# Weights turned in one pass, products of constants in TensorE's early waits, layer-norm pieces in other periods

## What is computed

```python
def _layernorm(x, axis=-1, eps=1e-05):
    m = jnp.mean(x, axis=axis, keepdims=True)
    v = jnp.var(x, axis=axis, keepdims=True)
    return (x - m) / jnp.sqrt(v + eps)
...
    Q = jnp.einsum('bnd,hdk->bhnk', x, proj_q)
    K = jnp.einsum('bmd,dk->bmk', x, proj_k)
    V = jnp.einsum('bmd,dv->bmv', x, proj_v)
    logits = jnp.einsum('bhnk,bmk->bhnm', Q, K)
    weights = jax.nn.softmax(logits, axis=-1)
    O = jnp.einsum('bhnm,bmv->bhnv', weights, V)
    Y = jnp.einsum('bhnv,hdv->bnd', O, proj_o)
...
    mid = jnp.einsum('amh,ehn->aemn', x, w1)
    out = jnp.einsum('aemn,enh->amh', mid, w2)
...
    xn = _layernorm(x, axis=-1)
    x = x + attention(xn) + ffn(xn)
```

## Time and profile before

| | us |
|---|---|
| median of 3 runs | 1669.87 |
| lowest, highest | 1668.98, 1670.22 |
| time of the profiled execution | 1669.67 |
| its span in the trace | 1667.9 |
| TensorE busy | 1634.7 |
| GpSimd busy | 1379.9 |
| ScalarE busy | 1304.2 |
| VectorE busy | 1239.3 |

### The profile page before, as it was taken

How to read it: one execution, slowest core, us unless ns; L and a number is a source line. 1 busy time by engine, 2 the same in 40 slices (tenths; PEclk the granted TensorE clock), 3 DMA queues, 4 the chain that set the end, 5 groups by cost and what they waited for, 6 DMA issues and landing times.

```text
span 1667.9 us, 46510 instructions
## 1 busy us (share of the span) xinstructions
PE 1634.7 (98%) x18820; PEld 1214.1 (73%) x18820; DVE 1239.3 (74%) x2655; ACT 1304.2 (78%) x1350; POOL 1379.9 (83%) x1008
## 2 busy tenths in 40 slices
PE   7999999999999999999999999999999999999998
PEld 6777777777777777777777777777777777777775
DVE  5777777777777777777777777777777777777775
ACT  4777877787787788778778777877878787787785
POOL 2788888888888888888888888888888888878876
PEclk9999999999999999999999999999999999999999
DMA  8000000000000000000000000000000000000000
GB/s 230 2 2 2 1 2 14 2 2 2 2 15 2 2 2 3 13 2 2 2 8 8 2 2 1 8 8 2 2 2 8 8 2 2 2 14 2 2 1 14
DMA packets 16769, 16.73 MB, mean 10 GB/s; under 512 B 432, under 2 KB 12976, under 8 KB 16560
## 3 DMA queue, kind: packets, MB, share of 16 engines
q1 hardware_dynamic: 15520, 13.24, 2.7%
q10 hardware_dynamic: 1040, 0.52, 0.1%
HBM read 9.57 MB, written 4.19 MB: 8 GB/s over the span
## 4 chain that ended last, share of the span: by engine, by line
POOL 56%; issue 24%; PE 18%; ACT 1%; DVE 0%; POOLq 0%; DMA 0%; SPq 0%; DVEq 0%; ACTq 0%
POOL pr_lo L306 40%; POOL xacc L318 9%; POOL xn L300 3%; PE s_ps L548 2%; PE s_ps L550 2%; PE s_ps L535 2%; PE t_ps L586 2%; PE t_ps L589 2%; PE t_ps L588 2%; POOL rstd L345 2%; POOL xacc L324 1%; POOL xn_lo L290 1%; PE s_ps L432 1%; PE s_ps L434 1%; PE s_ps L433 1%
## 5 line engine op out<-in xcount | busy, mean ns | idle before, releaser
L306 POOL TENSOR_TENSOR pr_lo<-pr,pr_hi 128x1024 f16<-128x1024 f32 x511 | 1086.4, 2134 | 264.3 <-ACT pr_hi L396 264.3
L389 ACT ACTIVATE pr<-s_ps,boost,scale 128x1024 f32<-128x1024 f32 x512 | 616.8, 1205 | 211.1 <-PE s_ps L550 210.3
L778 DVE TENSOR_REDUCE key_max<-s_ps 128x128 f16<-128x1024 f32 x512 | 624.0, 1219 | 0.0
L396 ACT ACTIVATE pr_hi<-pr 128x1024 f16<-128x1024 f32 x512 | 525.4, 1051 | 8.1
L548 PE MATMUL s_ps<-g_lo,xT 128*128 128x128 f16 x4096 | 512.4, 219 | 1.1 <-DVE g_lo L791 1.1
L550 PE MATMUL s_ps<-g_hi,xT 128*128 128x128 f16 x4096 | 512.3, 219 | 0.0
L548 PEld LDWEIGHTS s_ps<-g_lo,xT 128*128 128x128 f16 x4096 | 400.7, 98 | 31.6 <-DVE g_lo L791 1.6
L550 PEld LDWEIGHTS s_ps<-g_hi,xT 128*128 128x128 f16 x4096 | 400.8, 98 | 29.7
L586 PE MATMUL t_ps<-pr_hi,xn_hi 128*128 128x512 f16 x1024 | 388.7, 380 | 16.3 <-POOL pr_lo L306 14.4
L588 PE MATMUL t_ps<-pr_lo,xn_hi 128*128 128x512 f16 x1024 | 388.1, 379 | 0.0
L589 PE MATMUL t_ps<-pr_hi,xn_lo 128*128 128x512 f16 x1024 | 388.1, 379 | 0.0
(11 more groups left out here) (123 smaller groups left out, 1602.7 us busy)
## 6 DMA issues: line engine op xcount, KB each, us to landing
out_dram<-xacc SPq DMA_DIRECT2D x16, 256.0 KB, 2.3
w_sb<-in_L_ffn_w_dram SPq DMA_DIRECT2D x1, 2048.0 KB, 10.2
pr<-in_L_attn_proj_q_dram ACTq DMA_DIRECT2D x1, 512.0 KB, 4.7
xacc<-in_L_attn_x_dram SPq DMA_DIRECT2D x2, 256.0 KB, 5.1
pr<-in_L_attn_proj_o_dram SPq DMA_DIRECT2D x1, 512.0 KB, 6.5
xacc<-in_L_attn_x_dram SPq DMA_DIRECT2D x1, 384.0 KB, 11.0
xacc<-in_L_attn_x_dram SPq DMA_DIRECT2D x1, 128.0 KB, 6.3
wkv<-in_L_attn_proj_k_dram SPq DMA_DIRECT2D x1, 64.0 KB, 2.9
```

Of the source, the lines that this page charges most:

```text
L306: pool.tensor_tensor(pr_lo[:, u % RING, :], pr32[:, u % PR, :], pr_hi[:, u % RING, :], ALU.subtract)\
L389: act.activation(pr32[:, u % PR, :], both_banks(u), ACT.Exp, bias=boost[:, 0:1], scale=scale[:, 0:1])\
L396: act.activation(pr_hi[:, u % RING, :], pr32[:, u % PR, :], ACT.Copy).then_inc(p_hi_ready, 1)
L778: dve.tensor_reduce(key_max[:, u % 2, :], both_banks(u).rearrange("p (t q) -> p q t", q=P), AX_X, ALU.max).then_inc(keys_max, 1)
```

## The change

1. Turns: wq, wo and w1 are turned by `pe.transpose` with ident, which is one instruction in place of two. Since this no longer centres, wq is centred by VectorE (a copy of the first column, then a subtraction that also empties the bank), and F is centred once by a product in period 7. w1 is turned in periods 0 to 3 into one bank, emptied by ScalarE and VectorE in turn; all of F is folded in periods 4 and 5.
2. `keep_going`: 24 products of constants (6, 5, 8 and 5), 512 columns each, at four places of TensorE's queue ahead of the loop. Nothing reads their result.
3. Start-up order: a_hi is made for head 0 alone first; C is folded in two halves around the first scores; the emptying of wq's turn, the low part of the first tiles and others go to other engines or places; the first projection comes ahead of the second turn of x.
4. Layer norm of coming tiles: rstd in period 8p+8, normalise in 8p+9, xn_hi on ScalarE in 8p+10, xn_lo in 8p+11. Statistics have two slots. VectorE's pieces stay in their periods.

The core of the diff:

```diff
+        def ln_slot(tile):
+
+            return AHEAD + tile % 2
...
+            first_rstd(0)
+            first_rstd(1)
+            xn_low(0, 0, HT)
             xn_low(HT, HT, HT)
+            first_rstd(2)
...
-                if n % 8 == 2 and (tile := ln_tile(n // 8)) is not None:
-                    pool.wait_ge(ln_var, tile - AHEAD + len(FIRST_TILES) + 1)
-                    pool.tensor_tensor(rstd[:, AHEAD:AHEAD + 1], var_eps[:, AHEAD:AHEAD + 1],
-                                       minus_half[:, 0:1], ALU.pow).then_inc(ln_rstd, 1)
-                if n % 8 == 3 and (tile := ln_tile(n // 8)) is not None:
-                    normalise_next(tile)
-                if n % 8 == 7 and (tile := ln_tile(n // 8)) is not None:
-                    xn_low(tile, 0, 1)
+
+                if (tile := ln_tile(n // 8 - 1)) is not None:
+                    if n % 8 == 0:
+                        slot = ln_slot(tile)
+                        pool.wait_ge(ln_var, tile - AHEAD + len(FIRST_TILES) + 1)
+                        pool.tensor_tensor(rstd[:, slot:slot + 1], var_eps[:, slot:slot + 1], minus_half[:, 0:1], ALU.pow)\
+                            .then_inc(ln_rstd, 1)
+                    if n % 8 == 1:
+                        normalise_next(tile)
+                    if n % 8 == 3:
+                        xn_low(tile, 0, 1)
...
-                if n % 8 == 6 and (tile := ln_tile(n // 8)) is not None:
+                if n % 8 == 2 and (tile := ln_tile(n // 8 - 1)) is not None:
                     split_high(tile, 0, 1)
...
+            def keep_going(count):
+
+                for n in range(count):
+                    pe.matmul(sum_bank(0).rearrange("p (n c) -> p n c", c=P), ident16[:, :],
+                              ident16[:, :].unsqueeze(1).to_broadcast([P, 4, P]), start=True, stop=True)
+
             pe.wait_ge(consts, 7)
+            keep_going(6)
             pe.wait_ge(kv_in, 32)
...
-                last = pe.matmul(s_ps[:, h * P:(h + 1) * P], wq_sb[:, h, :], centre[:, :], start=True, stop=True)
-            last.then_inc(transposed, 1)
-            pe.wait_ge(o_in, 16)
-            for h in range(H):
-                last = pe.matmul(s_ps[:, N + h * P:N + (h + 1) * P], wo_sb[:, h, :], ident[:, :], start=True, stop=True)
+                last = pe.transpose(s_ps[:, h * P:(h + 1) * P], wq_sb[:, h, :], ident[:, :])
             last.then_inc(transposed, 1)
             pe.wait_ge(kv_ready, 1)
+            keep_going(5)
             pe.wait_ge(evacuated, 1)
...
                 for c in range(MC):
-                    last = pe.matmul(w1_turn(e)[:, c * P:(c + 1) * P], w1_sb[:, e, c * P:(c + 1) * P], centre[:, :],
-                                     start=True, stop=True)
+                    last = pe.transpose(sum_bank(W1_BANK)[:, c * P:(c + 1) * P], w1_sb[:, e, c * P:(c + 1) * P], ident[:, :])
                 last.then_inc(w1_turned, 1)
...
+                if n < 4 and rest:
+                    turn_w1(2 * n + place)
+                if n in FOLDS and rest:
+                    for e in range(2):
+                        fold_ffn(4 * FOLDS[n] + 2 * place + e)
...
+                if n == F_CENTRED:
+                    pe.wait_ge(f_copied, 1)
+                    pe.matmul(ffn_part(n), centre[:, :], f32w[:, :], start=True, stop=True).then_inc(f_ps, 1)
...
+            keep_going(8)
             row_of_amax(0, None)
             turn_tiles(0)
             spread_amax(0, None)
-            turn_w1(0)
-            turn_tiles(HT)
-            turn_w1(1)
+            keep_going(5)
             pe.wait_ge(weights_ready, 1)
             project(0)
-            turn_w1(2)
+            turn_tiles(HT)
+            fold_c(0)
...
+            wq_turned = s_ps[:, 0:N].rearrange("p (h d) -> p h d", h=H)
+            dve.wait_ge(transposed, 2)
+            dve.tensor_copy(wq_first[:, :], wq_turned[:, :, 0]).then_inc(wq_first_ready, 1)
+            dve.wait_ge(wq_first_ready, 1)
+            dve.tensor_tensor(wqT, wq_turned, wq_first[:, :].unsqueeze(2).to_broadcast([P, H, P]), ALU.subtract)\
+               .then_inc(evacuated, 1)
...
-                    dve.wait_ge(ln_xn32, tile)
-                    tile_mean(AHEAD)
+                    dve.wait_ge(ln_xn32, tile - 1)
+                    tile_mean(ln_slot(tile))
```

More of the change, by code:

```diff
@@ L279, in _, with first_rstd @@
             pool.memset(centre[0:1, 0:1], 0.0).then_inc(consts, 1)
-            for g, (first, count) in enumerate(FIRST_TILES):
+            def first_rstd(g):
+                first, count = FIRST_TILES[g]
                 pool.wait_ge(ln_var, g + 1)
@@ L364, in empty_w1, with high_of_a, empty_c @@
                 act.wait_ge(w1_turned, e + 1)
-                act.activation(w1T[:, e, :], w1_turn(e), ACT.Copy).then_inc(w1_evacuated, 1)
-            act.wait_ge(transposed, 2)
-            act.activation(wqT, s_ps[:, 0:N].rearrange("p (h k) -> p h k", h=H), ACT.Copy).then_inc(evacuated, 1)
+                act.activation(w1T[:, e, :], sum_bank(W1_BANK), ACT.Copy).then_inc(w1_evacuated, 1)
+            def high_of_a(first, count):
+                heads = a_ps.rearrange("p (h k) -> p h k", h=H)[:, first:first + count, :]
+                act.activation(a_hi[:, first:first + count, :], heads, ACT.Copy, scale=inv_scale[:, 0:1])\
+                   .then_inc(hi_ready, 1)
+            def empty_c(half):
+                act.wait_ge(folded, half + 2)
+                act.activation(c32[:, half * BANK:(half + 1) * BANK], c_ps(half), ACT.Copy).then_inc(c_copied, 1)
             split_high(0, 0, HT)
+            split_high(HT, HT, HT)
             act.wait_ge(transposed, 3)
             act.activation(woT, s_ps[:, N:2 * N], ACT.Copy).then_inc(evacuated, 1)
-            split_high(HT, HT, HT)
-            act.wait_ge(folded, 2)
-            act.activation(c32[:, :], s_ps[:, N:2 * N], ACT.Copy).then_inc(c_copied, 1)
             act.wait_ge(scales, 1)
[L376 to L379, removed]
+            high_of_a(0, 1)
             def g_high(k):
@@ L453, in _, with fold_c @@
             last.then_inc(folded, 1)
-            pe.wait_ge(evacuated, 2)
-            for n in range(2):
-                last = pe.matmul(s_ps[:, N + n * BANK:N + (n + 1) * BANK], wkvT[:, P:2 * P],
-                                 woT[:, n * BANK:(n + 1) * BANK], start=True, stop=True)
-            last.then_inc(folded, 1)
+            pe.wait_ge(o_in, 16)
+            for h in range(H):
+                last = pe.transpose(s_ps[:, N + h * P:N + (h + 1) * P], wo_sb[:, h, :], ident[:, :])
+            last.then_inc(transposed, 1)
+            def fold_c(half):
+                pe.wait_ge(evacuated, 2)
+                if half == 1:
+                    pe.wait_ge(xT_ready, NT)
+                pe.matmul(c_ps(half), wkvT[:, P:2 * P], woT[:, half * BANK:(half + 1) * BANK], start=True, stop=True)\
+                  .then_inc(folded, 1)
             def turn_tiles(first):
@@ L462, in turn_tiles @@
                 if first:
-                    pe.wait_ge(xT_ready, first)
+                    pe.wait_ge(evacuated, 2)
                 for t in range(first, first + HT):
                     at = (t - first) * 2 * P
-                    pe.transpose(turn16[:, at:at + P], xn_hi[:, t, :], ident16[:, :])
-                    last = pe.transpose(turn16[:, at + P:at + 2 * P], xn_lo[:, t, :], ident16[:, :])
+                    pe.transpose(first_turned(first)[:, at:at + P], xn_hi[:, t, :], ident16[:, :])
+                    last = pe.transpose(first_turned(first)[:, at + P:at + 2 * P], xn_lo[:, t, :], ident16[:, :])
                 last.then_inc(xT_ps, 1)
```

121 lines of the change are left out of this document (73 added, 48 removed).

## The result

| | before | after |
|---|---|---|
| median, us | 1669.42 (5 runs) | 1794.73 (5 runs) |
| lowest, highest | 1668.98, 1670.22 | 1794.48, 1795.64 |
| profiled execution, span in the trace | 1669.67, 1667.9 | 1795.64, 1793.9 |

The changed kernel takes 1.0751 times as long (95% interval 1.0736 to 1.0766): slower, by 125.3 us.

A forecast was written before the change was run, and what follows sets the result against it. TensorE, busy 1634.7 of 1667.9 us, was taken as the bound. 1669.7 + 116.4 (loop) + 16 (clock) - 2.5 (start-up) = 1799.6, and 0.2 up to the median: 1800 us, range 1768 to 1862.

The forecast's parts named there:

- A: The forecast itself: ACT's wait passes to TensorE, with few clock falls (0 to 15); 1784 to 1808 us, chance 0.57.
- all its signs: In the changed profile: copy waits, TensorE stalls released by ACT's exponential, no pr_lo wait, more GpSimd idle, longer pairs.
- The stall: In the loop: TensorE waits for ACT's exponential behind the copy xn_hi, 2.6 us once per pair, bounds 2.4 and 2.7.
- The deadline wait: TensorE's repeated wait for GpSimd's last pr_lo, 23.3 us in 52 places, goes because the stall moves the deadline.
- the shorter run on GpSimd: Ahead of TensorE's deadline, GpSimd's run loses rstd and wins xn_lo: about 0.12 shorter, alone at most 6.3 us won.
- The clock: In the loop: TensorE's new idles lower its clock between 0 and 54 times, 0 to 86 us; 10 falls, 16 us taken.
- The two rows it was taken from: Trace idles: after 1.77 us behind sparse work the clock fell to 0.50; after 1.84 behind dense work it stayed 1.00.
- Case B: Rival: the same stall, with the clock falling at most stalls, up to 1870 us; chance 0.28.
- The start-up: Ahead of the loop: first scores 4.9 us earlier, part given back by folding; net -2.5 us, between -6 and +1.
- The small rival: At the start: constant products do not keep the clock from falling, so 1.6 us are missing from the gain.
- D: Rival: GpSimd's run decides, not ACT, and TensorE never stands for the copy; 1661 us, at best 1644; chance 0.08.
- The range's low end: 1768 us: no clock falls (1784), the stall at 2.4 (-11) and the start-up at -6.

The follow-up runs named there:

- e3: The changed kernel with ScalarE's copy xn_hi one period later (n % 8 == 3), GpSimd's order as changed: 1660.65 us (0.9949).
- e4: The changed kernel with normalise ahead of the head add on GpSimd in the same period: 1748.42 us (1.0474).
- e5: The changed kernel with the copy xn_hi on ScalarE and xn_lo on GpSimd both at n % 8 == 4: 1644.75 us (0.9851).
- e2: The changed kernel with rstd, normalise, xn_lo and the copy xn_hi back in their old periods: 1667.88 us (0.9992).
- e7: The kernel of e5 without the 24 products of constants: 1647.44 us.
- e1: The kernel before with only the layer-norm pieces moved and the two slots added: 1797.22 us (1.0766).
- e8: The kernel of e5 with wq, wo and w1 turned by ordinary two-instruction products with ident: 1648.10 us.

## Why the prediction was right

The prediction was 1800 us, in a range of 1768 to 1862, with slower at 0.92. It was 1794.7: its likeliest case, A, with all its signs.

**The stall: right in place and size.** 2.60 us per pair was worked out, 2.60 is measured in the pair shown and 2.59 over all of them; 54 waits of 2.8 and some 150 us on ACT were named, 54 and 149.6 are in the waits. The working held because each link was a handover whose time stood in the trace before, and because ACT showed no idle at that place. e3 and e4 back it: take the copy out and 134 us go, take 0.7 from the chain and 0.69 per pair goes.

**The deadline wait: right.** The 23.3 us are gone, since the stall delays the deadline by more. The loop is +116.4 by the forecast and by the trace. That the shorter run on GpSimd would win some 0.12 per pair was right too: in e3 the deadline wait is 7.4 us less, 0.14 per pair. It is so little because xn_lo (0.448) takes the place of rstd (0.565) in that run; with xn_lo elsewhere as well (e5) all 0.45 are won.

**The clock: right in kind, too high in number.** 10 falls of 1.6 us were taken, for 16 us; 7 of 1.66 came, for 11.6. The two rows it was taken from, one that fell and one that did not, allowed anything from 0 to 54, and 10 was a choice: that it came so near 7 is luck. The second of these rows also ends at 1655.00, before TensorE goes on at 1655.15, so it doesn't show what came after the idle. The stretch behind it does, and bears the reading out:

```profile
1655.15:1660.00 4.85, 4.85 (x32) 2.61 (x33) 1.85 (x5) 0.00 (x0) 2.42 (x4) 1.00 0.00 0
```

By the Trainium skill, "TensorE: Matmul & The Clock Gate", section "Why this matters for your kernels", a mid-kernel gap of this length keeps the clock: 47 of 54 stalls agree with it, 7 do not. Case B (a fall at most stalls) is refuted for this stall.

**The start-up: right to 1 us, with one step missed.** First scores came at 20.27 instead of the 20.0 forecast, and periods 4 and 5 took 1.78 and 1.79 more, where 1.9 was said. The periods that the folding left gave 1.5 back (0.8 and 0.7), where 1.3 was said. Not foreseen were the 1.04 us of period 3, where the last turn of w1 and the row of maxima wait for the bank to be emptied and the scores stand behind them. So -1.8 in the profiled execution and -1.4 by the medians of e2, and not -2.5. The bounds, -6 to +1, held it. The small rival, that constant products don't hold the clock, is refuted by e7. The eight one-pass turns of wq are about 0.11 us apart, between the 0.06 and 0.18 that were said. The 0.18 of L443 was itself a mean of 0.213 and 0.11, on either side of 8.8 us.

**The other side, D,** had its decisive point right: normalise would have to end before 803.9, and it ends too late because the new queue has it behind pr_lo. e3 shows the figure that D would have given, 1661, by putting the copy where that point no longer matters.

The total is 5 us under the forecast: 4.4 less from the clock, 0.7 more from the start-up, and the rest between profiled execution and median (the profiled one was the longest of the five runs of after). The range's low end was summed a little low: its own terms, 1784 - 11 - 3.5, give 1769.5 and not 1768, which changes nothing.

## What to carry to other kernels

Before moving a small instruction on an in-order engine, look at what stands behind it and at what it waits for. Here a copy of 0.3 us waited for a piece that another engine could start only after work this engine had just released, with the next exponential behind it: that circle set 2.6 us per pair, and moving the copy by one period, behind that exponential, turned +7.5% into -0.5% (e3). With xn_lo moved too, and the copy where its input was long done and the next instruction had slack, it was -1.5% (e5). And an engine's idle time is room only for instructions whose result nobody is about to wait for.

## What the runs showed of the hardware that was not expected

- Stalls alike to 0.01 us (2.43 us of idle behind dense work, all but the first) lowered the granted clock in 7 of 54 cases, spaced nearly evenly, every seventh to ninth; e1 has seven as well, six to nine apart. Stalls some 0.7 us shorter (e4) did so in none of 54. What picks the seven stays open.
- A one-pass turn of float32 costs half of the product with the identity: in the groups of L525, 32 instructions of 282 ns instead of 64 of 284 (e8), and within a turn both follow each other 0.11 us apart.
- Products of constants in TensorE's waits at the start were worth 2.7 us (e7), more than the one fall of the granted clock. The 16 float32 products for A are spaced nearly twice as far without them (213 ns instead of 112), while the granted clock of that stretch reads 1.00. In all kernels looked at the spacing halves once in the first 14 us, and no stretch of the granted clock shows it. Ahead of its first change the record of the clock isn't to be relied on here; the spacing of products is. The timeline of e7 first, then its stretch (columns as above), then the timeline of e5:

```profile
10.10 3.75 PE L484 MATMUL s_ps<-wkvT,pr 128*128 128x128 f32 x16 [1.61 <-DVE pr L818]
```

```profile
8.00:12.00 4.00, 2.39 (x12) 2.02 (x11) 3.47 (x19) 0.00 (x0) 1.20 (x2) 1.00 1.08 370
```

```profile
9.33 2.05 PE L484 MATMUL s_ps<-wkvT,pr 128*128 128x128 f32 x16 [0.44 <-DVE pr L818]
```
